# A second graph layer whose gathers add on to resident rows, and one product per tile in place of two

## The reference

```python
def _layer(h, e_h, src, dst, iso_mask, norm, W_r, W_sl, W_el):
    self_msg = jnp.where(iso_mask[:, None], h @ W_el, h @ W_sl)
    msg = (e_h + h[src]) @ W_r
    agg = jax.ops.segment_sum(msg, dst, num_segments=h.shape[0])
    return rrelu(agg * norm + self_msg)
...
e_h = rel_embed[rel_id]
for W_r, W_sl, W_el in [(W_r1, W_sl1, W_el1), (W_r2, W_sl2, W_el2)]:
    h = _layer(h, e_h, src, dst, iso_mask, norm, W_r, W_sl, W_el)
```

## Time and profile before

| | us |
|---|---|
| median of 3 runs | 2828.49 |
| the 3 runs | 2828.49, 2805.66, 8008.05 |
| the profiled execution | 2798.32 |
| its span, first to last instruction | 2796.3 |

### The profile page before, as it was taken

The page is one execution under the profiler, slowest core; times in us unless marked ns, Lnnn a source line. Parts: engine busy times, 40 slices in busy tenths (PEclk is TensorE's granted clock), DMA queues, the critical chain, the costliest instruction groups (busy, mean ns, idle before and its releaser), DMA issues. The chain is left out here.

```text
span 2796.3 us, 48046 instructions
## 1 busy us (share of the span) xinstructions
PE 2280.0 (82%) x12452; PEld 1679.9 (60%) x12452; DVE 2046.6 (73%) x7945; ACT 1242.2 (44%) x2774; POOL 1472.9 (53%) x1597
## 2 busy tenths in 40 slices
PE   4777777776999778759999806888199999999997
PEld 3656666666999667747777605666044444444443
DVE  4887766766878668778888695666267878787785
ACT  2887666663333244446666400000044444444443
POOL 3433222305777677636555003777666666666662
PEclk9998778777999889979999857998599999999999
DMA  4776555545665799944444104565313232333321
GB/s 117 213 214 178 172 172 165 175 133 172 192 190 165 241 296 301 293 149 134 124 123 123 36 9 132 168 195 183 147 44 104 97 106 97 106 101 102 102 94 49
DMA packets 372812, 413.45 MB, mean 148 GB/s; under 512 B 51706, under 2 KB 260366, under 8 KB 372570
## 3 DMA queue, kind: packets, MB, share of 16 engines
q1 hardware_dynamic: 335002, 340.50, 38.6%
q0 software_dynamic: 34496, 69.37, 9.5%
q10 hardware_dynamic: 3072, 0.86, 0.1%
HBM read 264.05 MB, written 179.90 MB: 159 GB/s over the span
## 5 line engine op out<-in xcount | busy, mean ns | idle before, releaser
L570 POOL DMA_INDIRECT x_dst<-in_x_dram,idx x196 | 189.9, 969 | 382.7 <-DMA edge_x<-x_dst 308.0
L1737 PE MATMUL p_f<-nT,w 128*128 128x512 f32 x784 | 354.0, 594 | 0.0
L1750 PE MATMUL p_y<-g_T,w 128*128 128x512 f32 x784 | 352.8, 593 | 0.8 <-ACT yT L1769 0.8
L1781 ACT ACTIVATE g_T<-p_f,bf 128x512 f32<-128x512 f32 x392 | 261.5, 688 | 34.5 <-PE p_f L1737 34.2
L1140 POOL DMA_INDIRECT x_src<-x_rows,idx x196 | 185.6, 947 | 166.9 <-DVE normed L1307 73.3
L908 POOL DMA_INDIRECT h_src<-in_x_dram,idx x196 | 195.0, 995 | 135.2 <-POOLq L151 75.7
L1545 POOL DMA_INDIRECT x_rows<-xv,idx x196 | 211.1, 1077 | 86.6 <-issue 52.1
L620 PE MATMUL p_s<-tile_step,at_least 98*128 98x129 f32 x784 | 132.8, 322 | 142.9 <-DVEq L720 140.8
L1718 POOL TENSOR_TENSOR xs<-xs,bo_rows 128x512 f32<-128x512 f32 x98 | 127.2, 1298 | 215.4 <-DMA xs<-x_rows 188.1
L908 POOL DMA_INDIRECT h_src<-h_table,idx x196 | 192.2, 981 | 81.6 <-issue 57.4
L1737 PEld LDWEIGHTS p_f<-nT,w 128*128 128x128 f32 x784 | 142.1, 191 | 142.4 <-issue 119.7
(11 more groups left out here) (298 smaller groups left out, 6229.7 us busy)
## 6 DMA issues: line engine op xcount, KB each, us to landing
xs<-x_rows SPq DMA_DIRECT2D x98, 512.0 KB, 3.6
x_in<-in_x_dram SPq DMA_DIRECT2D x98, 256.0 KB, 3.4
h_table<-h_rows SPq DMA_DIRECT2D x98, 256.0 KB
x_rows<-x_in SPq DMA_DIRECT2D x98, 256.0 KB, 2.5
out_dram<-res SPq DMA_DIRECT2D x98, 256.0 KB, 2.0
x_rows<-x_rows SPq DMA_DIRECT2D x50, 500.0 KB
edge_x<-x_dst SPq DMA_DIRECT2D x98, 128.0 KB, 3.0
h_own<-edge_x SPq DMA_DIRECT2D x49, 256.0 KB, 4.4
```

Of the source, the lines that this page charges most:

```text
L570: e.indirect_dma_start(out=x_dst[:, m % PN, j, :], out_offset=None, in_=x, in_offset=bass.IndirectOffsetOnAxis(ap=idx[:, DST, 2 * m + j:2 ...
L1737: e.matmul(p_f[ch][:], w_1[:, ch * P:(ch + 1) * P], nT[:, s, :], start=True, stop=True)\
L1750: mm = e.matmul(p_y[:], w_2[:, ch, :], g_T[:, s, ch, :], start=(ch == 0), stop=(ch == FCH - 1))
L1781: e.activation(g_T[:, s, ch, :], p_f[ch][:], ACT.Gelu, bias=bf1[:, ch:ch + 1]).then_inc(gelu_ready, 1)
```

## The change

In layer 1 the indirect DMAs write to the tile's rows of e_h instead of h_src, and add there what they gather (compute_op add). h_src is allocated in layer 0 only. PE forms p_acc with one product per tile, of e_h. The waits are as they were, the one of POOL on acc_prod among them. Layer 0 is unchanged: its transfers have the operation bypass.

```diff
@@ -811,7 +811,7 @@
-                h_src = sb("h_src", [P, HN, GT, D], F32, c)
+                h_src = sb("h_src", [P, HN, GT, D], F32, c) if l == 0 else None
@@ -905,8 +905,9 @@
                         wait(e, src_used, g - HN + 1)
                         for j in range(GT):
                             t = g * GT + j
-                            e.indirect_dma_start(out=h_src[:, g % HN, j, :], out_offset=None, in_=(x, h1_table)[l],
-                                                 in_offset=bass.IndirectOffsetOnAxis(ap=idx[:, (SRC, H_SRC)[l], t:t + 1], axis=0))\
+                            e.indirect_dma_start(out=h_src[:, g % HN, j, :] if l == 0 else e_h[:, t, :], out_offset=None, in_=(x, h1_table)[l],
+                                                 in_offset=bass.IndirectOffsetOnAxis(ap=idx[:, (SRC, H_SRC)[l], t:t + 1], axis=0),
+                                                 compute_op=ALU.bypass if l == 0 else ALU.add)\
                                 .then_inc(gathered[g % HN], 16)
@@ -925,8 +926,7 @@
                                 else:
-                                    e.matmul(p_acc[g % 2][:, at], e_h[:, g * GT + j, :], mate[:, g % 2, at], start=True, stop=False)
-                                    mm = e.matmul(p_acc[g % 2][:, at], h_src[:, g % HN, j, :], mate[:, g % 2, at], start=False, stop=True)
+                                    mm = e.matmul(p_acc[g % 2][:, at], e_h[:, g * GT + j, :], mate[:, g % 2, at], start=True, stop=True)
```

## The result

The changed kernel takes 2898.97 us (median of 4 runs, 2884.68 to 2913.66), the kernel before 2817.07 us beside it. The ratio is 1.0315, 95% interval 1.023 to 1.040: slower by 82 us. Forecast were 2905 us and 76 us more.

The account below looks back on a forecast made before the run. The prediction took the DMA engines to bound the second layer's stage. Transfers +81 less 5 us free gave +76: 2874 us for the profiled execution, 2905 us for a median, range 2812 to 3090 us.

Parts of the forecast that it names:

- Pace of the kernel before: Second layer's stage, 303 us: runs at the pace of the DMA engines, busy 0.98; PE is waited for 1.6 us.
- The buffer and the wait on acc_prod: h_src not allocated in layer 1, gathers still wait on acc_prod six groups back, so run no further ahead: 0.
- The transfers, costed at +81 us: Layer-1 gathers: each row a packet of its own with two reads, +0.41 us a gather over 196 gathers.
- The 83 ns: Engine time per accumulated row in layer 1: two hardware-queue packets of 41.5 ns, against 31 ns a row now.
- the POOL term: Layer-1 gather issue on POOL: +59 us at 1420 ns each, beside the DMA cost, only the larger counting.
- rival C: POOL's issue of layer-1 gathers becomes the bound: +59 us, 2887 us; chance included in the forecast's 0.40.
- the DMA term: Layer-1 accumulating transfers on the DMA engines: +81 us, the term said to decide.
- The slack of 34 us: POOL's room in layer 1: 9.2 us waiting for PE plus 25 us behind its last gather, 0.17 us a gather.
- the prediction's own sum: Second layer's stage: transfers' 81 us less some 5 us the DMA engines have free, +76 us, nothing off for PE.
- rival D: PE's clock falls to 1.2 GHz throughout and PE bounds layer 1: +55 us, 2883 us; chance included in the forecast's 0.40.

Follow-up runs that it names:

- the half change: Kernel before with tiles 0 and 2 of each layer-1 group accumulating into e_h, 1 and 3 gathered plainly with two products: 2858.8 us, ratio 1.018.
- run 253: Not a run's label: the first layer's gathers run 253 us from first to last on the chip where the kernel before takes 2806 us.

## Why the prediction was right, and which step of it was not

The forecast of 2905 us holds (2899, and +76 against +82), but the term that carries it was not the one that acts; that the number holds is luck. Part of the closeness of 2905 lies in the runs too: 2874 us were forecast for a profiled execution and 31 more for a median, while here the profiled one took 2913.7, 15 above its median.

- *Pace of the kernel before.* That PE is off the path was right: one product a tile with plain gathers gains nothing (1.007, on the slower chip), and in the changed kernel PE falls to 58% for no gain. That the DMA engines alone set the pace was argued and not shown. DVE's 43 us of waiting for stores speak for it; no run took the load away on the chip with the short steps.
- *The buffer and the wait on acc_prod.* 0, as said: POOL waits for it 1.8 us in all.
- *The transfers, costed at +81 us.* Their form was right, a row as a packet of its own. The size was off: a row with its two reads takes 69 ns, not 83, so 0.32 and not 0.41 us more a gather, 63 us of engine time and not 81. The 83 ns were twice the mean of the hardware queue's packets, 41.5 ns, and that mean mixes packets of 512 bytes at 29 ns with ones of 2048 bytes at 90 and of 4 at 9; twice a packet of a row's size would be 59 ns. And it lies beside the POOL term: taking a quarter of the engines' load away left the gathers at 363.6 us, and plain transfers at the same beat cost as much. The Trainium skill (Collectives: The Full Stack, section The bandwidth ceiling: the fold count and why AG ≠ RS ≠ AR) has the rule that the two source reads of an add halve the rate. The trace comes near it, 0.57 us for 0.25 or 2.3 times, though here each row also became a packet; and the rule sizes a term that does not decide.
- *POOL's instruction, rival C.* This is the step that failed. I set 1420 ns for the case of three descriptors instead of two, argued from the scatter (987 ns) that it was unlikely, and took the DMA term as the larger. It is 1558 ns in the mean. With the formula of the prediction 196 x (1.558 - 0.981) - 34 = +79 us, where the stage grew by 83.5. The slack of 34 us was read nearly right, 31 of it went: the distance from the last gather to the last product shrank from 28.4 to 4.9 us, and the wait for PE from 9.2 to 1.8.
- *The size.* 79 us by POOL and 76 by DMA are near each other by accident. With the transfers as measured the prediction's own sum would be 63 - 5 = 58 us, for a stage that grew by 83.5. The sizes alone would not settle it, though, nor does the half change, whose +25 us both sums give (23 and 26). What tells the two apart are the kernel with its copies moved away and the one with the memset.
- *PE's clock, rival D.* It fell, from 0.92 to 0.80 (0.83 between 985 and 1185 us), and no cost of it shows: PE waits 144 us for the gathers.

## What to carry to other kernels

Here work that moved into a DMA was paid on the engine that issues it, in a longer instruction. Before such a change, compare that engine's beat with the step (here 4 x 1.25 = 5.0 us of 5.44) and its slack per instruction; 0.17 us was all there was for an addition of 0.58. Where two resources both look full afterwards, imitate the cost of each in the old kernel: a memset of the right length told what the profile with its DMA share of 0.95 could not. Look at what the stand-in slows besides, as this one slowed DVE. And before a variant is said to tell two causes apart, work out what each would give with the sizes as measured: the half change fits both.

## What the runs showed of the hardware that I had not expected

- The accumulating gather of 128 rows of 512 bytes keeps POOL 1.54 us (median) where the plain one takes 0.94 to 0.95, in every run and on every chip here, and sends 144 packets instead of 32: each row by itself, where a plain gather puts eight rows in one packet.
- Beside a memset of 128x704 f32 on POOL, 706 ns long, DVE's mate took 895 ns in the mean instead of 368, and up to 1548.
- The chips differ by 9% on the same kernel (2806 and 3063 us), and not evenly. The first layer's gathers run 253 us from first to last on the one and 323 us on the other, the attention's 307 and 357, while the accumulating gathers of layer 1 take 363 to 364 us on both: what POOL paces is the same everywhere, and the change costs 75 to 85 us on the one chip, and on the other 385.1 - 331.7 = 53 us (both with the copies moved). In the kernel before with its copies moved, what waits for p_acc starts late there. These are rows of PE and POOL in order of time, then waits of DVE and POOL:

```profile
1207.44 0.39 PE L929 MATMUL p_acc<-mate,h_src 128*128 128x128 f32 x2
...
1209.88 0.94 POOL L908 DMA_INDIRECT h_src<-h_table,idx  x1 [1.17 <-remote]
```
```profile
DVE accT L1050 <- remote: 44.2, 31, 1.5
POOL h_src L908 <- remote: 36.2, 32, 1.2
```

The last product ends at 1207.83 us by the model, and POOL's next gather, which waits for its semaphore, starts 2 us later; the second fence has the waits of 1150 to 1350 us, by a releaser that the trace does not name. Whether the products there really end later than the profile draws them, or their signal comes late, no run tells.
